# Row sums of softmax: four key tiles added by three chained DMAs and one product with ones, instead of two DMAs and four half products

## What is computed

```python
h = _layernorm(x) * (scale + 1.0) + shift
q, k, v = split(h @ w_qkv)
q = _apply_rope(_layernorm(q, q_norm_w), position)
k = _apply_rope(_layernorm(k, k_norm_w), position)
scores = einsum('bhqe,bhke->bhqk', q, k) / sqrt(e)
attn = softmax(scores)
o = einsum('bhqk,bhke->bhqe', attn, v)
x + (o @ w_out) * gate
```

## Time and profile before

| | us |
|---|---|
| median of 3 runs | 1744.09 (1743.22 to 1744.54) |
| the profiled execution | 1738.36 |
| its span, first to last instruction | 1736.6 |
| busy: PE, DVE, ACT, POOL | 1669.5, 1247.1, 1034.1, 680.7 |
| mean granted TensorE clock | 0.988 of full |

### The profile page before, as it was taken

How to read it: one execution, slowest core, us unless ns; L and a number is a source line. 1 busy time by engine, 2 the same in 40 slices (tenths; PEclk the granted TensorE clock), 3 DMA queues, 4 the chain that set the end, 5 groups by cost and what they waited for, 6 DMA issues and landing times.

```text
span 1736.6 us, 34608 instructions
## 1 busy us (share of the span) xinstructions
PE 1669.5 (96%) x13350; PEld 1007.4 (58%) x13350; DVE 1247.1 (72%) x1667; ACT 1034.1 (60%) x1610; POOL 680.7 (39%) x707
## 2 busy tenths in 40 slices
PE   5978899999999999999999999999999999999887
PEld 3734556665666666666566666666656666665444
DVE  8767677777777777777777777777777777776553
ACT  3445666666666666566666666666666666665552
POOL 0523243344344344334434434433443443443322
PEclk9979999999999999999999999999999999999999
DMA  6034355554645555555555555555555546454553
GB/s 214 25 68 85 82 129 113 134 116 110 137 113 125 125 122 119 119 127 117 122 125 126 112 130 117 119 131 116 122 116 126 131 107 143 104 113 107 128 122 110
DMA packets 55432, 204.48 MB, mean 118 GB/s; under 512 B 6872, under 2 KB 6872, under 8 KB 39144
## 3 DMA queue, kind: packets, MB, share of 16 engines
q0 software_dynamic: 18144, 132.13, 39.1%
q1 hardware_dynamic: 37128, 70.14, 12.0%
HBM read 53.25 MB, written 16.88 MB: 40 GB/s over the span
## 4 chain that ended last, share of the span: by engine, by line
PE 92%; DVE 5%; issue 1%; DMA 1%; POOL 1%; ACT 0%; SPq 0%; ACTq 0%; DVEq 0%; POOLq 0%
PE O L459 13%; PE SA L440 13%; PE Y L345 12%; PE Y L358 10%; PE Y L348 9%; PE Y L352 9%; PE Y L475 8%; PE SM L397 6%; PE MB L380 3%; PE SA L444 3%; PE SA L335 1%; PE SA L418 1%; DVE cst L1074 1%; DVE cst L1066 1%; PE MB L408 1%
## 5 line engine op out<-in xcount | busy, mean ns | idle before, releaser
L819 ACT ACTIVATE probs<-SM 128x1024 f32<-128x1024 f32 x256 | 262.3, 1025 | 235.1 <-PE SM L444 226.3
L1066 DVE TENSOR_REDUCE cst<-SM 128x2 fp32r<-128x1024 f32 x236 | 289.1, 1225 | 153.4 <-PE MB L397 153.4
L1315 POOL DMA_DIRECT2D probs<-probs x126 | 109.8, 871 | 594.0 <-ACT probs L821 541.1
L1066 DVE TENSOR_REDUCE cst<-MB 128x2 fp32r<-128x1024 f32 x236 | 287.0, 1216 | 0.0
L459 PE MATMUL O<-probs,vals 128*32 128x512 f32 x2048 | 270.9, 601 | 0.0
L1296 POOL TENSOR_TENSOR pair_part<-rows,rope_pair 128x256 f32<-128x256 f32 x128 | 119.6, 935 | 382.8 <-DVE rows L1043 381.9
L821 ACT ACTIVATE probs<-SA 128x1024 f32<-128x1024 f32 x256 | 262.4, 1025 | 0.0
L345 PE MATMUL Y<-wqkv_hi,hT_hi 128*128 128x512 f32 x716 | 215.4, 423 | 0.0
L715 ACT ACTIVATE rows<-Y 128x512 f32<-128x512 f32 x121 | 72.4, 599 | 205.0 <-PE Y L352 205.0
L348 PE MATMUL Y<-wqkv_hi,hT_lo 128*128 128x512 f32 x716 | 193.9, 392 | 0.5 <-DVE hT_lo L1049 0.5
L1055 DVE SCALAR_TENSOR_TENSOR qk_lo<-MB,pass_w,qk_hi 128x512 fp32r<-128x512 f32 x128 | 90.3, 746 | 144.8 <-ACT qk_hi L751 144.7
(11 more groups left out here) (221 smaller groups left out, 3557.0 us busy)
## 6 DMA issues: line engine op xcount, KB each, us to landing
probs<-probs POOLq DMA_DIRECT2D x126, 1024.0 KB, 7.7
xin<-in_x_dram SPq DMA_DIRECT2D x62, 256.0 KB, 7.4
xres<-in_x_dram SPq DMA_DIRECT2D x60, 256.0 KB, 2.6
out_dram<-xres SPq DMA_DIRECT2D x60, 256.0 KB, 5.7
shift_scale<-mod_rows SPq DMA_DIRECT2D x15, 512.0 KB, 3.7
gate<-mod_rows SPq DMA_DIRECT2D x16, 256.0 KB, 5.4
rows<-in_L_cond_mod_w_dram SPq DMA_DIRECT2D x2, 1024.0 KB, 9.0
probs<-in_L_cond_w_qkv_dram SPq DMA_DIRECT2D x2, 1024.0 KB, 13.3
```

What stands on the lines that cost most here:

```text
L819: act.activation(probs[:, a, 2:4, :], SM[:], ACT.Exp).then_inc(s_exp, 1)
L1066: dve.tensor_reduce(heads[:, 2 * half:2 * half + 2, 0], bank[:], AX.X, ALU.max, negate=True).then_inc(max_out, 1)
```

## The change

The partial sums are replaced by one total. The DMAs for t = 1, 2 and 3 all add to the buffer of key tile 0, one after the other: each waits until the one before has landed. There are 189 of them, where there were 126. The third DMA of group s is issued at the head of step s+1, the second in the middle of POOL's list for step s. One product with ones of 512 columns for four heads stands in place of the four of 256 columns. ACT takes the logarithm straight from `Y`, between the two exponentials of key tile 2 of the next step. The copies `move_first_sum` and DVE's `add_sums` are gone. Buffers rotate by one from group to group, and the exponentials of tiles 0 to 2 of the next group wait for the DMA that read their buffer, those of tile 3 for the product with ones.

```diff
     def probs_buffer(g, t):
-        return t ^ (g % 2)
+        return (t + g) % TT
...
-            def add_over_keys(g, t, h):
+            def add_over_keys(g):
...
+                pe.wait_ge(keys_added, 16 * 3 * (g + 1))
                 for i in range(HG):
-                    mm = pe.matmul(Y[head_rows(i), cols], ones_r[:, 0:E].bitcast(F32),
-                                   probs[:, probs_buffer(g, t), i, cols],
+                    mm = pe.matmul(Y[head_rows(i), :], ones_r[:, 0:E].bitcast(F32),
+                                   probs[:, probs_buffer(g, 0), i, :],
                                    start=True, stop=True, skip_group_check=True)
...
-                    add_over_keys(s - 1, 2, 1)
+                    else:
+                        pe.wait_ge(v_out, s + 5)
+                    add_over_keys(s - 1)
                 weigh_values(s, 1)
...
+                    if g > 0 and t < TT - 1:
+                        act.wait_ge(pv_step, TT * (g - 1) + t + 2)
+                        act.wait_ge(keys_added, 16 * (3 * (g - 1) + t + 1))
+                    elif g > 0:
+                        act.wait_ge(ones_done, g)
...
                 key_exponentials(s, 2, 0)
+                if s > 0:
+                    log_sums(s - 1, Y[:])
                 key_exponentials(s, 2, 1)
...
             def add_keys(g, t):
                 pool.wait_ge(s_exp, 2 * (TT * g + t) + 2)
-                pool.wait_ge(pv_step, TT * g + t)
-                pool.dma_start(probs[:, probs_buffer(g, t - 1)].rearrange("p h n -> p (h n)"),
+                pool.wait_ge(pv_step, TT * g + 1)
+                if g > 0 or t > 1:
+                    pool.wait_ge(keys_added, 16 * (3 * g + t - 1))
+                pool.dma_start(probs[:, probs_buffer(g, 0)].rearrange("p h n -> p (h n)"),
                                probs[:, probs_buffer(g, t)].rearrange("p h n -> p (h n)"), accum_op=ALU.add
...
             for s in range(LAST + 1):
+                if s > 0:
+                    add_keys(s - 1, 3)
...
                 add_keys(s, 1)
                 if tile(s + 5):
                     rotate(s + 5, 0)
+                if s < LAST - 1:
+                    add_keys(s, 2)
                 if s > 0:
                     scale_o(s - 1)
                 if tile(s + 5):
                     rotate(s + 5, 1)
                 if s == LAST - 1:
                     output_low(s - 4)
-                add_keys(s, 3)
+                    add_keys(s, 2)
                 if s - 5 >= 0:
                     add_residual(s - 5)
```

More of the change, by code:

```diff
@@ L566, in _ @@
                 if s > 0:
[L567 to L571, removed]
                     weigh_values(s - 1, 3)
@@ L577, in _ @@
                 if s > 0 and tile(s + 4):
-                    pe.wait_ge(first_summed, 2 * s)
+                    if s > 1:
+                        pe.wait_ge(sum_ln, s - 1)
+                    if tile(s + 5):
+                        pe.wait_ge(raw_out, raw_count(s + 5, 1))
                     project(s + 4, 2, Y[:])
@@ L585, in _ @@
                     scores_by_query_half(s + 1, 1, 0)
[L586 to L589, removed]
                 weigh_values(s, 0)
@@ L601, in _ @@
                     pe.wait_ge(o_low, n + 1)
-                    pe.wait_ge(sum_added, 2 * s - 1)
+                    pe.wait_ge(sum_ln, s - 1)
+                    if tile(s + 4):
+                        pe.wait_ge(v_out, s + 5)
+                    if s == LAST:
+                        pe.wait_ge(y_gated, NT - TT - 1)
                     project_out(n, Y[:], 0, 4)
@@ L634, in _ @@
                     scores_by_query_half(s + 1, 3, 0)
-                if group(s + 1):
-                    if tile(s + 6):
-                        pe.wait_ge(raw_out, raw_count(s + 6, 0))
-                    add_over_keys(s, 0, 0)
                 weigh_values(s, 2)
@@ L767, in output_high, with log_sums @@
                 act.activation(o_hi[:], tile_out(n), ACT.Copy).then_inc(o_high, 1)
-            def move_first_sum(g, h):
-                act.wait_ge(ones_done, 4 * g + h + 1)
+            def log_sums(g, sums):
+                act.wait_ge(ones_done, g + 1)
                 if g > 0:
@@ L774, in move_first_sum @@
                     act.wait_ge(parts_out, 3)
-                cols = half_cols(h)
-                act.activation(sum_inv[:, cols], Y[:, cols], ACT.Copy).then_inc(first_summed, 1)
-            def log_sums(g, sums):
-                if g < LAST:
-                    act.wait_ge(sum_added, 2 * g + 2)
-                else:
-                    act.wait_ge(ones_done, 4 * g + 1)
-                    act.wait_ge(o_scaled, g)
                 act.activation(sum_inv[:], sums, ACT.Ln).then_inc(sum_ln, 1)
@@ L1075, in late_maxima @@
                                   ).then_inc(max_out, 1)
-            def add_sums(g, h):
-                dve.wait_ge(ones_done, 4 * g + 3 + h)
-                dve.wait_ge(first_summed, 2 * g + 1 + h)
-                cols = half_cols(h)
-                dve.tensor_tensor(sum_inv[:, cols], sum_inv[:, cols], Y[:, cols], ALU.add).then_inc(sum_added, 1)
             def apply_gate(n, bank, to):
@@ L1228, in _ @@
                     late_maxima(s + 1, 1, 0)
-                if s > 0:
-                    add_sums(s - 1, 0)
                 if late(s + 1):
@@ L1243, in _ @@
                     inverse_roots(s + 7)
-                if s > 0:
-                    add_sums(s - 1, 1)
                 if tile(s + 5):
```

57 lines of the change are left out of this document (14 added, 43 removed).

## The result

The changed kernel takes 1760.79 us (median of 4 runs, 1755.51 to 1764.06), the kernel before 1744.16 us (4 runs). The ratio is 1.0093, 95% interval 1.0067 to 1.012: 16.6 us slower, where 50 us less were forecast. The profiled execution took 1755.51 us, with a span of 1753.7; against the one of before (1738.36) that is 17.1 us more, so the two traces hold the whole difference.

What follows compares the result with a forecast made beforehand. PE was taken to bound the middle steps, 25.54 us each. Savings of 53.6 + 0.5 + 0.5 - 4.4 = 50.2 us took the profiled 1738.36 to 1688.2; 5.7 for the median gave 1693.9, range 1685 to 1712.

Steps and rivals of the forecast that it cites:

- PE's part: In each of steps 1 to 57, four half-width products (1.82 us) give way to one wide (0.88), saving 0.94 us.
- Those gains count in full: Behind scores of tiles 1 and 3 and mid-step, projections of some 3 us cover PE, so nothing saved is lost.
- The head of the step: At `scores_by_query`, low parts come 0.13 us before PE; gain counted in full, chance 0.08 of losing 0.45 us a step.
- The loop of 23.7 us: Three chained DMAs with their waits: 8.1 + 7.9 + 7.5 + 0.2 us against a step of 24.6, so not binding.
- 4 us of slack: The third DMA lands 9.4 us into the next step; the product with ones wants it at 13.9.
- The rival of the hard chain: Three landings of 8.8 us make 26.6 us against 25.54 a step: 60 us more, 1804 us; chance 0.06.
- POOL goes on meanwhile: Between second and third DMA, POOL's issue, `scale_o`, second `rotate`, `add_residual` and `output_low` take 7.9 us in all.
- Late steps: Steps 58 to 63: step 58 gains 0.5 us, later ones lose 4.4 us, between 2 and 9, mostly through DMA landings.
- `move_c` holds PE in step 61: `scale_o` queues behind the second DMA in step 60, so `output_high` ends late and holds up `move_c`: 0.7 us.
- wait for the sums in step 62: The chain's last landing slips to 14.8 us into step 62, so PE waits there: 1.1 us.
- step 63: `add_residual` moves behind the second DMA in step 62, delaying this step 1.15 us; the wide call adds 0.43.
- three signs of being wrong: PE idle in middle steps, landings averaging over 8.2 us, or late steps losing more than 9 us.

Runs made afterwards that it cites:

- quarter DMAs: The changed kernel with each chained DMA moving one head of four (256 KB instead of 1 MB) and a small bias in the logarithm; 1742.8 us, ratio 0.9989.

## Why the prediction was wrong, point by point

- **PE's part: right in size, wrong in worth.** The wide product takes 0.88 us, as the earlier trace rows said (682.47 to 683.35), and the half calls are gone.
- **"Those gains count in full" is the step that failed.** It looked at what stands behind the half calls (projections) and not at the instruction two places behind each, `scores_by_query`, which waits for `s_exp`, as the row of the order ahead of the prediction says. The profile of before shows no wait there, because the half call covered it: a wait of zero has an owner all the same. Three half calls were worth 0.13 us each and not 0.455, the fourth was paid. The sum for a step is 0.0 and not -0.94. The quarter DMAs show it without the chain: steps 5 to 57 are 0.5 us shorter than before and not 50. This is the largest part, by far, of the 67 us by which the forecast was off; the chain adds 9.9 us in the same steps.
- **The head of the step, where "0.13 us of cover is left"**, looked for the right thing at the wrong signal: the low parts were in time, the exponential was not.
- **The loop of 23.7 us, which "does not bind".** Wrong mostly by what stands between the landings. The sum has 23.0 us for three of them (8.1, 7.4, 7.5) and 0.7 for all the rest; measured are 23.6 (7.86 each) and 3 x 0.57 = 1.7. So the loop is 25.3 us on average and 25.6 in a run of long landings, against a step that stayed at 25.5. Its 4 us of slack held for one landing, and a run of long ones uses them up. The rival of the hard chain was to decide at a mean landing of 8.46 us; with 0.57 us behind each it decides at 7.94 (an estimate, 25.54 / 3 - 0.57), and the measured mean is just below. With that the chain binds in spells, for 9.9 us in the middle steps and not for 60.
- **"POOL goes on meanwhile"**: not counted was that POOL's work, placed directly behind a DMA issue, holds DVE's `normalize_x`; 2.7 us in the middle steps, by the trace.
- **Late steps**, a net loss of 3.9 us forecast for steps 58 to 63 (4.4 - 0.5), for reasons of the chain: measured 8.6. Of its terms, `move_c` holds PE in step 61 (0.55 us, forecast 0.7); PE does not wait for the sums in step 62; step 63 is 0.4 us longer and not 1.6 (with quarter DMAs it is 2.8 shorter, and the whole chain puts 3.2 on top). Most of the 8.6 us goes with the lower clock, which the prediction did not consider there.
- Of the forecast's three signs of being wrong only the first came, middle steps with PE idle. Landings average 7.9 us and not over 8.2, and the late steps lost 8.6 us and not over 9: the other two would have passed a chain that binds. The weight given to a slower kernel, 0.06, was too small, since the case "the half calls were hidden anyway" was not among the rivals at all. With it, the chain needed to cost only a fifth of a per cent to make the kernel slower.

## What to carry to other kernels

Before counting a removed piece of work as gain, find the next instruction on its engine that waits for another engine, and measure from the start of the work that feeds that wait, not from the wait that the profile shows; a piece is free as far as it stands in such a gap. Spread over several gaps, small pieces cost less than one large piece in a single gap of the same size. A chain of transfers that fills nearly a whole step has no slack to recover with: a long landing reaches the engines some steps on, and a saving elsewhere brings the step nearer to the chain. Count what stands between a landing and the next issue, here 0.57 us, as well as the landings.

## What the runs showed of the hardware

- VectorE and GpSimd hold each other up. L997, which reads two tensors in SBUF, takes 0.74 us when GpSimd is idle (step 20 of the changed kernel), 1.12 with the middle DMA issued later, 2.7 with it issued right ahead of `scale_o`, and up to 3.35. The Trainium skill, SBUF — State Buffer, "SBUF: two separate sides", says that a VectorE operation with two inputs in SBUF and a GpSimd operation that reads SBUF take a shared pair of ports by an exclusive lock. The trace agrees in kind. By that section whoever starts first holds the ports for one whole instruction; in the rows of step 30 above L997 is recorded as starting before GpSimd's `scale_o` and L1250, and ends after both. The case that the prediction cited from that section, VectorE keeping GpSimd from issuing a DMA, did not show: the issue has a median of 0.87 us in both kernels.
- An accumulating 1 MB DMA lands in 7.0 us at best and 11.0 at the worst; where three follow one another in each step the mean is 7.9 us, where two stand apart 7.7 (middle steps of after and before). The next one, if it waits for the landing, starts 0.57 us after it. With 512 KB the median is 5.1 us, with 256 KB 3.8.
- Small groups of products between others of another tile shape are dear: two full products placed alone between narrow ones take 0.66 us and not 0.46, and two of the four products of `scores_by_query` placed alone, with a full product next, take as long as all four, 0.43 us.
- The granted clock can fall in single late steps (0.81 in step 62 of the changed kernel) while the same instructions run at 1.00 in another kernel (quarter DMAs): 26.6 us for the step against 22.6. Why was not settled.
